# A router's softmax in a fused decoder layer: negated logits, the exponential per tile with a bias, and the sum taken on ScalarE

## The reference

```python
h = jax.nn.gelu(ri @ r1_w.T + r1_b, approximate=False)   # ri: the row and six statistics of it
probs = jax.nn.softmax(h @ r2_w.T, -1)                   # 4096 tokens x 32 experts
topp, topi = jax.lax.top_k(probs, 2)
wnorm = topp / topp.sum(-1, keepdims=True)
...
score = jnp.where(routed, probs, -jnp.inf)
idx = jnp.argsort(-score, axis=0)[:cap].T                # each expert takes its 160 best tokens
```

## Time and profile before

| what | value |
|---|---|
| median of three runs | 1654.29 us |
| the profiled execution, its own time | 1652.59 us |
| its span, first to last instruction | 1650.8 us |
| mean granted clock of TensorE | 0.944 |
| TensorE matmuls busy | 1465.0 us, 89% of the span |
| VectorE busy | 930.8 us, 56% |
| ScalarE busy | 501.9 us, 30% |
| GpSimd busy | 311.7 us, 19% |

### The profile page before, as it was taken

One profiled execution on the slowest core, in us unless ns is written; L12 is line 12 of the kernel. 1 busy time (PEld: TensorE's weight loads), 2 busy tenths in 40 slices (PEclk: granted clock), 3 DMA queues, 4 the chain that ended last, 5 costly groups with the idle time before them and its releaser, 6 DMA issues.

```text
span 1650.8 us, 29327 instructions
## 1 busy us (share of the span) xinstructions
PE 1465.0 (89%) x10876; PEld 1127.5 (68%) x10912; DVE 930.8 (56%) x2750; ACT 501.9 (30%) x1191; POOL 311.7 (19%) x399
## 2 busy tenths in 40 slices
PE   5679999898888712799999999999999999999994
PEld 2356556556556411788788787887888878888783
DVE  8667999999989889332423324233242333423364
ACT  4556676675755652001001010010100101001023
POOL 4012121121112200112121121211212112121135
PEclk9689999999999755899999999999999999999998
DMA  6203213122220270176776777767767687676796
GB/s 179 71 28 95 77 65 115 55 81 71 81 74 2 102 312 32 50 294 237 277 275 220 295 246 264 283 215 295 255 251 288 210 300 262 238 293 219 289 341 200
DMA packets 92576, 311.04 MB, mean 188 GB/s; under 512 B 42838, under 2 KB 46940, under 8 KB 83164
## 3 DMA queue, kind: packets, MB, share of 16 engines
q1 hardware_dynamic: 79260, 287.87, 47.6%
q0 software_dynamic: 13248, 22.29, 6.0%
HBM read 273.18 MB, written 36.96 MB: 188 GB/s over the span
## 4 chain that ended last, share of the span: by engine, by line
PE 71%; DVE 17%; ACT 5%; issue 4%; POOL 1%; DMA 1%; DVEq 0%; POOLq 0%; ACTq 0%
PE bank L1045 38%; PE banks L1059 15%; PE bank L670 5%; PE banks L1062 4%; DVE arena L1478 3%; PE banks L772 2%; DVE arena L1940 2%; DVE arena L1468 1%; PE bank L672 1%; ACT arena L1209 1%; PE banks L783 1%; ACT arena L1140 1%; DVE arena L1518 1%; PE banks L753 1%; PE bank L800 1%
## 5 line engine op out<-in xcount | busy, mean ns | idle before, releaser
L1412 ACT ACTIVATE arena<-bank 128x160 f32<-128x160 f32 x288 | 87.4, 304 | 870.6 <-PE bank L1045 868.7
L1045 PE MATMUL bank<-keep,arena 128*128 128x160 f32 x2304 | 320.0, 299 | 1.9 <-DVE arena L2144 1.9
L1045 PE MATMUL bank<-arena 128*128 128x160 f32 x2304 | 319.8, 301 | 0.9 <-issue 0.9
L1045 PEld LDWEIGHTS bank<-keep,arena 128*128 128x128 f32 x2304 | 315.4, 189 | 5.8 <-issue 3.2
L1045 PEld LDWEIGHTS bank<-arena 128*128 128x128 f32 x2304 | 316.0, 191 | 4.2 <-issue 4.2
L2144 DVE TENSOR_TENSOR arena<-arena,bank 128x160 f32<-128x160 f32 x256 | 82.2, 321 | 405.4 <-ACT arena L1412 352.8
L1059 PE MATMUL banks<-arena 128*128 128x512 f32 x576 | 252.4, 592 | 0.0
L2331 POOL DMA_INDIRECT acc_rows<-arena,keep x64 | 102.9, 1607 | 630.0 <-DVE arena L2089 611.9
L1059 PEld LDWEIGHTS banks<-arena 128*128 128x128 f32 x576 | 107.6, 190 | 122.5 <-issue 122.5
L2087 DVE TENSOR_SCALAR arena<-banks,keep 128x512 f32<-128x512 f32 x32 | 24.0, 750 | 189.1 <-PE banks L1062 185.4
L670 PE MATMUL bank<-arena 128*128 128x512 f32 x224 | 104.4, 608 | 6.5 <-DVE arena L1478 6.5
(11 more groups left out here) (293 smaller groups left out, 1787.0 us busy)
## 6 DMA issues: line engine op xcount, KB each, us to landing
arena<-in_wup SPq DMA_DIRECT2D x32, 4096.0 KB, 12.4
arena<-in_wdn SPq DMA_DIRECT2D x32, 2048.0 KB
arena<-in_aup SPq DMA_DIRECT2D x32, 512.0 KB, 11.6
arena<-in_xT SPq DMA_DIRECT2D x32, 256.0 KB, 2.9
arena<-in_kT SPq DMA_DIRECT2D x8, 1024.0 KB, 5.6
arena<-in_v SPq DMA_DIRECT2D x32, 256.0 KB, 6.4
x_rows<-arena SPq DMA_DIRECT2D x8, 1024.0 KB, 4.4
acc_rows<-arena SPq DMA_DIRECT2D x8, 1024.0 KB, 6.8
```

What stands on the lines that cost most here:

```text
L1045: m = pe.matmul(u[:, g * CAP:(g + 1) * CAP], w, xeT[e.slot][:, c, :], start=(c == 0), stop=(c == C - 1))
L1412: act.activation(sg[k], Ub[k][:, 0:CAP], ACT.Silu).then_inc(up_a(f"silu{j}"), 1)
```

## The change

ScalarE now writes the logits with the opposite sign into `lg` (a factor of -1 in the copy, in `router_3` and in `last_logits`). VectorE takes the smallest of these for each token, which is minus the largest logit, and nothing more. ScalarE takes the exponential straight from `lg`, by four activations of 128x32, one per tile, each with the factor -1, with that tile's column of `nmx` as its bias, and with the running sum over the 32 experts, written to `wsum`. The subtraction and the sum on VectorE are gone; the reciprocal, the product and `top_two` stand as before. In the list of steps `lmin` takes the place of `lmax` and `lsub`, and `lsum` is gone; who waited for `lsub` now waits for `lmin`. Nothing else moves: apart from these instructions every engine's queue holds the same work in the same order.

```diff
-        so_v = steps("softmax_vector", ["lmax", "lsub", "lsum", "lrec", "prob", "top", "at",
+        so_v = steps("softmax_vector", ["lmin", "lrec", "prob", "top", "at",
                                        "cast", "oh", "ohs", "save", "rec2", "w"])
...
             def router_3(b):
                 act.wait_ge(*ro_t.at("lg", b))
-                act.wait_ge(*so_v.at("lsub", b - 1))
-                act.activation(lg, Wb[0][:, 0:TB * NE].rearrange("p (a e) -> p a e", a=TB), ACT.Copy)\
+                act.wait_ge(*so_v.at("lmin", b - 1))
+                act.activation(lg, Wb[0][:, 0:TB * NE].rearrange("p (a e) -> p a e", a=TB), ACT.Copy, scale=-1.0)\
                     .then_inc(ro_a("lg"), 1)
...
             def last_logits(b):
                 act.wait_ge(*rl_t.at("lg", b0))
-                act.wait_ge(*so_v.at("lsub", b - 1))
-                act.activation(lg, Pp[:, 0:TB * NE].rearrange("p (a e) -> p a e", a=TB), ACT.Copy).then_inc(rl_a("lg"), 1)
+                act.wait_ge(*so_v.at("lmin", b - 1))
+                act.activation(lg, Pp[:, 0:TB * NE].rearrange("p (a e) -> p a e", a=TB), ACT.Copy, scale=-1.0).then_inc(rl_a("lg"), 1)
...
             def router_4(b):
-                act.wait_ge(*so_v.at("lsub", b))
-                act.activation(pr, pr, ACT.Exp).then_inc((rl_a if b.off == NB - 1 else ro_a)("exp"), 1)
+                act.wait_ge(*so_v.at("lmin", b))
+                for tb in range(TB):
+                    m = act.activation(pr[:, tb, :], lg[:, tb, :], ACT.Exp, scale=-1.0, bias=nmx[:, tb:tb + 1],
+                                       accum_out=wsum[:, tb:tb + 1])
+                m.then_inc((rl_a if b.off == NB - 1 else ro_a)("exp"), 1)
...
             def softmax_1(b):
                 dve.wait_ge(*(rl_a.at("lg", b0) if b.off == NB - 1 else ro_a.at("lg", b)))
                 dve.wait_ge(*so_v.at("w", b - 1))
-                dve.tensor_reduce(nmx, lg, AX.X, ALU.max).then_inc(so_v("lmax"), 1)
-                dve.wait_ge(*so_v.at("lmax", b))
-                dve.tensor_tensor(pr, lg, nmx.unsqueeze(2).to_broadcast([P, TB, NE]), ALU.subtract)\
-                    .then_inc(so_v("lsub"), 1)
+                dve.tensor_reduce(nmx, lg, AX.X, ALU.min).then_inc(so_v("lmin"), 1)
 
             def softmax_2(b):
                 dve.wait_ge(*(rl_a.at("exp", b0) if b.off == NB - 1 else ro_a.at("exp", b)))
-                dve.tensor_reduce(wsum, pr, AX.X, ALU.add).then_inc(so_v("lsum"), 1)
-                dve.wait_ge(*so_v.at("lsum", b))
                 dve.reciprocal(wsum, wsum).then_inc(so_v("lrec"), 1)
```

## The result

The changed kernel took 1658.04 us (median of eight runs, 1656.73 to 1659.4), the kernel before 1653.26 (eight runs on the same chip, 1652.71 to 1654.54). The ratio is 1.0028, with a 95% interval from 1.0019 to 1.0037: **4.8 us slower**. The profiled execution took 1656.73 us; its span is 1654.9 us, 4.1 more than before.

What follows compares the result with a forecast made beforehand. The chain to TensorE was taken to pass through ScalarE's softmax exponentials in seven of eight executions. Five times +0.71 (+3.55), +1.02 and +0.38 made +4.95 us on 1654.29: 1659.2 us, range 1656.2 to 1662.5.

Steps and rivals of the forecast that it cites:

- five crossings: Four step ends and batch 5's softmax, where TensorE waits for decays queued behind ScalarE's exponential; together +3.55 us.
- I = 0.31 us: Time from one exponential's start to the next on ScalarE with a running sum; bounds 0.22 and 0.50.
- Rival 1: On ScalarE the accumulator read hides under the next activation, 0.22 us or less between starts; +2.3 us, 1656.6; chance 0.17.
- rival 2: On ScalarE the read stands whole behind each activation, 0.50 us between starts; +10.3 us, 1664.6; chance 0.05.
- +0.71 at each crossing: From VectorE's reduction to line 1209, 0.85 us before would become 1.56, and TensorE would get it whole.
- The first softmax costs nothing: Near 196.65 us, +0.71 would go into 1.1 us of slack before TensorE's broadcast: 0.
- Closing stage +1.02 and +0.38: Second to last softmax delays the gelu's table load by 1.02 us; the last delays its reciprocal by 0.38.
- VectorE's gain arrives nowhere: VectorE's two dropped instructions per softmax only lengthen its wait for line 1097, 0.94 to about 1.4 us, at step ends.
- Rival 3, the clock: One or two more retention stretches at TensorE's lower clock, 1.96 us each, 1661 to 1663 in all; chance 0.12.
- The signs of being wrong: Exponentials 0.22 us apart, TensorE's step-end idle growing less than the exponentials, or a retention stretch taking another time than before.
- The base: Starting point of the forecast: median 1654.29 us; the profiled execution, 1652.59, would take 1657.5.

Runs made afterwards that it cites:

- the move: Softmax exponentials moved behind decays for head 2 of the next step (batch 5: behind heads 4 to 7): changed kernel 1652.88 us, kernel before 1652.07 us.
- doubling: The changed kernel with each softmax's four exponentials taken twice, the first four into buffers later overwritten: 1669.63 us, ratio 1.0099 to the kernel before.
- the first experiment: The changed kernel with the exponentials' running sum removed and the sum back on VectorE: 1656.51 us, ratio 1.0021 to the kernel before.

## Why the prediction was right

The forecast was 1659.2 us and slower; 1658.04 came, inside the range. The mechanism is as predicted; that the total comes so close (4.95 us forecast, 4.8 measured) is in part luck, since one term was too large and three effects of the clock nearly cancel. By its own steps:

- **The chain passes through the softmax at five crossings.** Shown, by the waits (0.46 to 1.13, 0.55 to 1.14, and in batch 5 0.73 to 1.41) and by the move, with which the changed kernel loses 0.8 us against the kernel before instead of 4.8.
- **I = 0.31 us.** Right: 0.31 in the trace, 0.305 by doubling. Rival 1 (0.22) is what happens without the sum, as the first experiment shows, and rival 2 (0.50) does not happen, since the read lies over two activations.
- **+0.71 at each crossing.** The crossing itself grew by 0.69, the undisturbed steps by 0.54 to 0.68, in the mean 0.63. Five of these are 3.1, not 3.55. The trace shows 3.6 because the third step end had a stretch at the lower clock, worth about 0.5: of its 1.69 us, 1.1 fell into TensorE's wait, which is gone there. The match of the sum is thus better than that of its term. The missing 0.08 is small shifts: at the fourth step end, which grew least, the reduction came 0.13 sooner after the preceding broadcast (63.22, not 63.35) and the broadcast 0.02 sooner after line 1209; what moved the reduction is not shown.
- **The first softmax costs nothing.** Right, -0.03; doubling used up the slack there.
- **Closing stage +1.02 and +0.38.** Measured 0.98 and 0.37, and +1.45 when these two alone are changed.
- **VectorE's gain arrives nowhere.** Right in the total. The figure for its wait was wrong: ahead of the statistics in the next step it grew from 0.94 to 2.25, not to 1.4. I had added what VectorE saves, about 0.5, and left out that line 1097, for which it waits, comes 0.7 later too.
- **Rival 3, the clock.** Neither away nor decisive: +0.5 at the third step end, +0.5 in line 865, -1.3 at the experts' start, where the rival gave 2 to 4 us on top of the forecast. Its net effect in this one pair of traces is about -0.3, and it differs from one execution to the next. The rival's price was wrong: it set the 5.40 us against the 3.44 of the next group, but the same group takes 3.71, so a stretch costs 1.69 and not 1.96, and only 0.5 of that reached the end where TensorE had a wait behind it.
- **The signs of being wrong.** One of them came: a stretch of retention took another time than before, and so TensorE's wait, which was to be about 1.2 at all four step ends, is gone at the third. The experts were to be unchanged but for their start, and were 1.3 us shorter.
- **The base.** The profiled execution was to take 1657.5 and took 1656.73. The forecast of the median started from 1654.29, the median of three runs; eight runs gave 1653.26. From there 4.95 makes 1658.2. Most of the miss of 1.2 us is this base.

What stays open: why one kernel's times fell into two groups 3.5 us apart, why moving batch 5's exponential goes with slower lines 818 and 858, and why the changed crossings go with a slowed retention at the third step end.

## What to carry to other kernels

Ask who stands behind an instruction in its engine's queue before giving that engine more work: ScalarE was idle for six microseconds ahead of the exponential, and still each 0.1 us added there reached TensorE, because the next activation in the queue was the one TensorE wanted. Four small activations with a running sum cost four whole durations; one large one and a sum on an engine with time to spare was cheaper here, and putting the instruction behind the one that is waited for was worth more than either form. Before trusting a difference of a microsecond or two, look at which stretches of TensorE's work the clock slowed in each trace.

## What the runs showed of the hardware

- An activation with a running sum gives up the overlap with the next: starts 0.31 us apart at 128x32, 0.22 without the sum.
- At 32 columns an activation with a bias from a column takes as long (309 ns) as one of 128 columns with a constant (310 ns).
- TensorE's stretches at a granted clock of 0.50 do not stay in place between executions of one program. In five profiles of the same kernel line 670 was slowed at the fourth, the third, the second or no later step end. One such stretch, 5.40 us for 3.71, cost 1.7 us where TensorE had no wait ahead of line 631, and 0.5 where a wait of 1.1 us took most of it.
- The first softmax in these five profiles began at 196.5 to 198.0 us, before anything that was edited: 1.5 us of scatter come from the program's start.
